# Graph network in four layers: the leaky step of the attention scores on ScalarE, products of high parts first on TensorE, and GpSimd's bias additions held until the aj columns

## The chip, the cores and the metric

The kernel runs on one core of a Trainium2 chip. The metric is the device time of one execution in microseconds (us), as the median of several runs. Engines are named as in the profile: PE (TensorE, matmul), PEld (its weight loads), DVE (VectorE), ACT (ScalarE), POOL (GpSimd), SP (SyncE, which issues the DMAs here).

## The reference

16 graphs of 1024 nodes with 256 features, a dense float32 matrix `adj` of 1024 x 1024 for each, and four layers, each followed by a layer norm of x plus its result:

```python
# layer 0 touches the first 25 nodes of each graph (five small groups), before the loop
# layer 1: attention; z = x @ W.T + bW
ai = z @ wai.T + bai; aj = z @ waj.T + baj          # one number per node each
e = ai + aj.T                                       # 1024 x 1024
e = where(e >= 0, e, 0.2 * e)                       # the leaky step
att = where(adj > 0, e, -9e15)
att = softmax(concat([att, -1e9]), -1)[:, :n]       # a sink column beside the row
x = layernorm(x + att @ z)
# layer 2: x = layernorm(x + relu(((1 + eps) * x + adj @ x) @ W1 + b1) @ W2 + b2)      hidden 512
# layer 3: x = layernorm(x + silu(rmsnorm((eps * x + adj @ x) @ W1 + b1)) @ W2 + b2)   hidden 1024
```

## The kernel before, in words

Each engine has its own program, written out by hand in `layers`, and they meet through semaphores. Every engine runs its instructions in order, so an instruction that waits holds all that stand behind it. Graphs are done one after another in `graph(b, ...)`; the attention scores of graph b + 1 are computed while PE works on layers 2 and 3 of graph b.

Nodes are tiled in 8 tiles of 128 (`NT`), features in 2 (`DT`), and the 1024 nodes of an output in two halves of 512 (`h`). For nearly float32 results most operands are split into a high part (rounded to `F32R`, taken by ACT, or by POOL for some tiles) and a low part (the rest, subtracted by DVE or POOL), and a product is three matmuls: high x high, high x low, low x high. `agg_step` (L755 to L757) adds tile k of `adj @ x` to two banks, `hidden_tile` (L795) makes one 128-wide tile of a hidden layer, `second_step2` (L806) and `second_step3` (L820) multiply the hidden tiles by W2 of layers 2 and 3. A half goes through agg (bank), `agg_hi` on ACT (`a_hi`), `agg_lo` on DVE (`a_lo`, L1276), hidden tiles, then in layer 2 `relu` on ACT (L1006), the second step, then `residual`, `statistics`, `normalize` on DVE with `rstd_of` on POOL, then `x_high` on ACT (L990) and `x_low` on POOL (L1141), which the next layer's aggregation waits for. Two banks hold hidden tiles, so tile m waits for the relu (layer 2) or the squares (layer 3) of tile m - 2.

The scores of graph b + 1 start with `attention_sums` on DVE (L1327, two sums per tile, the last four tiles right after the normalization of the second half) and `attention_columns`, which gives the columns aj (L1333) and ai. PE's `aj_rows` (L733) turns aj into rows in two banks, `aj_copy` (L1269, L1270) copies them and 0.2 times them to SBUF. For each of 8 row tiles `score_mask` (L1343) makes the mask of the adj tile into `neg_mask`, which is the memory of `scratch`; one instruction (L1355) makes the leaky step, max(0.2 aj + shift, aj), with ai taken out of the row; L1360 adds the mask and takes the row maximum; `negated_top` (L1367) negates it with the floor; ACT's `exp` (L994) follows, and PE's `turn_att` (L706) transposes the result. The order on DVE around it is: aj_copy, three rows of scores, `agg_lo` of layer 2's second half, and the other rows between the residuals, statistics and normalizations of layer 2.

On POOL, `add_bias` (L1147) adds layer 2's bias to x, in the order: x_low of tiles 4 to 7, add_bias of tiles 0 to 3, `diag_gap` (L1173, the diagonal for layer 3), add_bias of 4 to 7, `diag_lo` (L1177) twice. ACT's `diag_hi` (L986) stands between; relu of the second half waits for diag_lo, whose source has the same memory.

Of the kernel before, what the change touches and what calls it, by code (L numbers as in the profile page):

```python
# [11 lines left out]
P = 128  # L12
# [438 lines left out]
def layers(nc, sb, sem, banks, ident, ones, WT_hi, WT_lo, W12_hi, W12_lo, W13_hi, W13_lo,  # L451
# [26 lines left out]
    neg_mask = scratch  # L478
# [6 lines left out]
    aj_row, aj_row2 = sb("aj_row", [P, NODES]), sb("aj_row2", [P, NODES])  # L485
# [6 lines left out]
    shift, floor = sb("shift", [P, NT]), sb("floor", [P, NT])  # L492
# [35 lines left out]
    s_sums, s_ai, s_aj, s_shift = sem("attention_sums"), sem("ai_columns"), sem("aj_columns"), sem("shift_and_floor")  # L528
# [85 lines left out]
    with nc.Block() as block:  # L614
# [81 lines left out]
        def _(pe):  # L696
# [44 lines left out]
            def x_ready(b, layer, k):  # L741
                pe.wait_ge(s_x_lo, x_count(b, layer - 1, k))

            def agg_step(b, layer, k, h, second_bank=None, ds=range(DT)):
# [3 lines left out]
                for d in ds:  # L748
# [7 lines left out]
                    nc.tensor.matmul(dst[:], hi, mt_lo[:, k, cols], start=False, stop=False)  # L756
                    mm = nc.tensor.matmul(dst[:], lo, mt_hi[:, k, cols], start=False, stop=done)  # L757
# [5 lines left out]
            def a_ready(b, layer, h):  # L763
                pe.wait_ge(s_a_lo, DT * agg_count(b, layer, h))

# [18 lines left out]
            def hidden_tile(b, layer, h, m):  # L784
# [7 lines left out]
                cols = slice(m * P, (m + 1) * P)  # L792
                for d in range(DT):
                    for n, (l, r) in enumerate(((w_hi, a_hi), (w_hi, a_lo), (w_lo, a_hi))):
                        mm = nc.tensor.matmul(hid_bank[i % 2][:], l[:, d, cols], r[:, d, :], start=(d == 0 and n == 0),  # L795
                                              stop=(d == DT - 1 and n == 2))
# [14 lines left out]
            def second_step3(b, h, m):  # L811
# [3 lines left out]
                pe.wait_ge(s_hid_lo[h], b * HT3 + m + 1)  # L815
                hi, lo = hid_hi[:, m % 4, :], hid_lo[:, m, :]
                for t in HALF_TILES:
                    cols = slice(t * P, (t + 1) * P)
                    for n, (l, r) in enumerate(((hi, W23_hi), (hi, W23_lo), (lo, W23_hi))):
                        mm = nc.tensor.matmul(out_bank[t // 2][:, t % 2 * D:(t % 2 + 1) * D], l[:, cols], r[:, m, :],  # L820
                                              start=(m == 0 and t % 2 == 0 and n == 0),
                                              stop=(m == HT3 - 1 and t % 2 == 1 and n == 2))
                    if m == HT3 - 1 and t % 2 == 1:
                        mm.then_inc(s_out, 1)
# [26 lines left out]
            def graph(b, first, last):  # L851
# [46 lines left out]
                for h in range(2):  # L898
                    a_ready(b, 2, h)
# [13 lines left out]
                a_ready(b, 3, 0)  # L913
# [14 lines left out]
                a_ready(b, 3, 1)  # L928
# [19 lines left out]
        def _(act):  # L948
# [88 lines left out]
            def graph(b, buf, first, last):  # L1037
# [32 lines left out]
                for m in range(HT2):  # L1070
                    relu(b, 0, m)
                    if m == 0:
                        diag_hi(b, 1)
                agg_hi(b, 2, 1)
                if not last:
                    for t in range(2):
                        exp(b + 1, t)
                for m in range(HT2):
                    relu(b, 1, m)
                    if m == 0 and not last:  # L1080
                        exp(b + 1, 2)
                for t in tiles(0):
                    x_high(b, 2, t, buf)
                if not last:
                    exp(b + 1, 3)
                    exp(b + 1, 4)
                for t in tiles(1):
                    x_high(b, 2, t, buf)
                if not last:
                    exp(b + 1, 5)  # L1090
# [27 lines left out]

            for t in range(NT):
                exp(0, t)  # L1120
# [11 lines left out]
        def _(pool):  # L1132
# [51 lines left out]
            def graph(b, buf, first, last):  # L1184
# [28 lines left out]
                for t in tiles(1):  # L1213
                    x_low(b, 1, t, buf)
                for t in range(NT):
# [35 lines left out]
        def _(dve):  # L1251
# [13 lines left out]
            def aj_copy(b):  # L1265
                for i in range(2):
                    dve.wait_ge(s_turned[i], turn_aj_use(b) + 1)
                    cols = slice(i * HALF, (i + 1) * HALF)
                    nc.vector.tensor_copy(aj_row[:, cols], turn_bank[i][:])  # L1269
                    nc.vector.tensor_scalar(aj_row2[:, cols], turn_bank[i][:], SLOPE, None, ALU.mult)\  # L1270
                      .then_inc(s_turn_free[i], 1)
# [60 lines left out]
            def attention_columns(b):  # L1332
                nc.vector.tensor_scalar(aj[:], qj[:], c_cols[:, 1:2], None, ALU.add).then_inc(s_aj, 1)  # L1333
                nc.vector.tensor_scalar(ai[:], qi[:], c_cols[:, 0:1], None, ALU.add).then_inc(s_ai, 1)
                dve.wait_ge(s_ai, b + 1)
                nc.vector.tensor_scalar(shift[:], ai[:], SLOPE - 1.0, None, ALU.mult)
                nc.vector.tensor_scalar(floor[:], ai[:], -1.0, SINK, ALU.mult, ALU.add).then_inc(s_shift, 1)

            def score_mask(b, t):
                dve.wait_ge(s_att_in[t], (b + 1) * 16)  # L1340
                if t > 0:
                    dve.wait_ge(s_masked, b * NT + t)
                nc.vector.tensor_scalar(neg_mask[:], att[:, t, :], 0.0, MASKED, ALU.is_le, ALU.mult).then_inc(s_mask, 1)  # L1343

            def scores(b, t, masked=False):

                if not masked:
                    score_mask(b, t)
                own = att[:, t, :]
                if t == 0:  # L1350
                    dve.wait_ge(s_shift, b + 1)
                    for i in range(2):
                        dve.wait_ge(s_turn_free[i], turn_aj_use(b) + 1)
                dve.wait_ge(s_mask, b * NT + t + 1)
                nc.vector.scalar_tensor_tensor(out=own, in0=aj_row2[:], scalar=shift[:, t:t + 1],  # L1355
# [213 lines left out]
```

## Time and profile before

| | |
|---|---|
| median of 3 runs | 2935.29 us (2935.02 to 2937.99) |
| the profiled execution | 2933.81 us, span 2932.0 us |
| PE busy | 2720.4 us, 93% |
| DVE busy | 2271.9 us, 77% |
| ACT busy | 1433.9 us, 49% |
| POOL busy | 1316.1 us, 45% |
| mean granted clock of PE | 0.973 |

The span is from the first to the last instruction. A busy share is that of the span in which the engine executes. The waits of PE for other engines show what lies beside its work.

### The profile page before, as it was taken

The numbers are of one execution on the slowest core, as the hardware profiler recorded it, in microseconds if no ns is written. First come the engines' busy times: TensorE is split into PE (matmuls) and PEld (weight loads), VectorE is DVE, ScalarE is ACT, GpSimd is POOL, SyncE is SP. The second block draws the span as 40 slices with busy tenths as digits, with TensorE's granted clock in tenths as the row PEclk, the third lists the DMA queues.
The fourth block names the chain that finished last, engine by engine and source line by source line (L and its number), as shares of the span: only waits on it lengthen the run. The fifth ranks groups of instructions, "written<-read, shape, count | busy, mean of one in ns | idle before, by whom it ended". The sixth has DMA issues, their size and how long they took to land.

```text
span 2932.0 us, 41513 instructions
## 1 busy us (share of the span) xinstructions
PE 2720.4 (93%) x14794; PEld 2292.7 (78%) x14794; DVE 2271.9 (77%) x4709; ACT 1433.9 (49%) x2772; POOL 1316.1 (45%) x1392
## 2 busy tenths in 40 slices
PE   3819999999999999999999999999999999999997
PEld 3707787888878787887878788887878788787886
DVE  3265889797878879787887979788887979788734
ACT  0223463746455473646456374645547364544624
POOL 1103455444535544454545544463554435454442
PEclk8958999999999999999999999999999999999999
DMA  4024031120404022030403112040402203040200
GB/s 139 1 78 129 1 110 35 57 88 1 144 1 144 1 80 65 21 124 1 144 1 105 41 52 93 1 144 1 144 1 79 66 19 126 1 144 1 65 9 15
DMA packets 205502, 181.06 MB, mean 62 GB/s; under 512 B 17617, under 2 KB 186993, under 8 KB 205297
## 3 DMA queue, kind: packets, MB, share of 16 engines
q1 hardware_dynamic: 197728, 177.06, 18.8%
q10 hardware_dynamic: 7568, 1.34, 0.3%
q8 instruction: 119, 1.95, 0.3%
q14 instruction: 87, 0.70, 0.1%
HBM read 161.17 MB, written 17.19 MB: 61 GB/s over the span
## 4 chain that ended last, share of the span: by engine, by line
PE 41%; DVE 38%; ACT 6%; issue 6%; POOL 2%; DMA 1%; SPq 0%; DVEq 0%; POOLq 0%; ACTq 0%
PE bank L795 12%; PE bank L820 8%; DVE stat L1304 5%; PE bank L755 5%; PE bank L757 4%; PE bank L756 4%; DVE att L1355 4%; DVE att L1360 4%; PE bank L706 3%; DVE sq_sum L1327 3%; DVE x_even L1319 3%; DVE x_odd L1319 3%; DVE mt_lo L1262 2%; DVE scratch L1343 2%; POOL rstd L1136 2%
## 5 line engine op out<-in xcount | busy, mean ns | idle before, releaser
L755 PE MATMUL bank<-mt_hi,x_hi 128*128 128x512 f32 x1536 | 639.7, 416 | 1.8
L757 PE MATMUL bank<-mt_hi,x_lo 128*128 128x512 f32 x1536 | 606.5, 395 | 0.0
L756 PE MATMUL bank<-mt_lo,x_hi 128*128 128x512 f32 x1536 | 604.6, 394 | 0.0
L1136 POOL TENSOR_TENSOR rstd<-ve,neg_half 128x4 f32<-128x4 f32 x128 | 147.6, 1153 | 499.3 <-DVE ve L1312 499.3
L755 PEld LDWEIGHTS bank<-mt_hi,x_hi 128*128 128x128 f32 x1536 | 291.9, 190 | 77.9 <-POOL x_lo L1141 20.9
L757 PEld LDWEIGHTS bank<-mt_hi,x_lo 128*128 128x128 f32 x1536 | 291.0, 189 | 65.4
L1388 DVE TENSOR_TENSOR sq_sum<-sq_sum,scratch 128x512 f32<-128x512 f32 x224 | 154.7, 691 | 232.1 <-ACT scratch L1025 232.1
L756 PEld LDWEIGHTS bank<-mt_lo,x_hi 128*128 128x128 f32 x1536 | 292.7, 191 | 49.5
L795 PE MATMUL bank<-a_hi,W_hi 128*128 128x512 f32 x768 | 319.5, 416 | 11.9 <-DVE a_lo L1276 11.4
L820 PE MATMUL bank<-W_hi,hid_hi 128*128 128x256 f32 x1024 | 294.7, 288 | 24.8 <-DVE hid_lo L1392 19.1
L795 PE MATMUL bank<-a_hi,W_lo 128*128 128x512 f32 x768 | 304.4, 396 | 0.0
L994 ACT ACTIVATE att<-att,neg_top 128x1024 f32<-128x1024 f32 x128 | 147.2, 1150 | 320.9 <-DVE neg_top L1367 319.9
L795 PE MATMUL bank<-a_lo,W_hi 128*128 128x512 f32 x768 | 304.1, 396 | 0.0
L820 PE MATMUL bank<-W_hi,hid_lo 128*128 128x256 f32 x1024 | 286.7, 280 | 0.0
L820 PE MATMUL bank<-W_lo,hid_hi 128*128 128x256 f32 x1024 | 286.4, 280 | 0.0
L1141 POOL TENSOR_TENSOR x_lo<-x_even,x_hi 128x256 fp32r<-128x256 f32 x192 | 181.3, 959 | 209.1 <-ACT x_hi L990 209.1
L963 ACT ACTIVATE mt_hi<-bank 128x512 fp32r<-128x512 f32 x256 | 153.4, 599 | 245.3 <-PE bank L720 245.2
L1141 POOL TENSOR_TENSOR x_lo<-x_odd,x_hi 128x256 fp32r<-128x256 f32 x192 | 178.1, 942 | 166.0 <-ACT x_hi L990 165.9
L1016 ACT ACTIVATE hid<-bank,b 128x512 f32<-128x512 f32 x256 | 176.4, 689 | 149.0 <-PE bank L820 103.6
L1262 DVE TENSOR_TENSOR mt_lo<-bank,mt_hi 128x512 fp32r<-128x512 f32 x256 | 173.0, 684 | 72.9 <-ACT mt_hi L963 72.8
L1030 ACT ACTIVATE hid<-hid 128x512 f32<-128x512 f32 x256 | 161.2, 630 | 137.2 <-DVE hid L1404 135.5
L806 PE MATMUL bank<-W,hid 128*128 128x256 f32 x1024 | 226.2, 379 | 0.0
(150 smaller groups left out, 6253.4 us busy)
## 6 DMA issues: line engine op xcount, KB each, us to landing
att<-in_adj SPq DMA_DIRECT2D x128, 512.0 KB, 7.8
adj_col<-in_adj SPq DMA_DIRECT2D x256, 256.0 KB, 3.0
out<-x_even SPq DMA_DIRECT2D x64, 128.0 KB, 2.9
out<-x_odd SPq DMA_DIRECT2D x64, 128.0 KB, 2.8
x_even<-in_x SPq DMA_DIRECT2D x56, 128.0 KB, 4.7
x_odd<-in_x SPq DMA_DIRECT2D x56, 128.0 KB, 3.7
G<-in_L_gnn_W SPq DMA_DIRECT2D x2, 2560.0 KB, 14.2
W_f<-in_L_gnn_W SPq DMA_DIRECT2D x1, 1024.0 KB, 8.6
```

What stands on the lines that cost most here:

```text
L755: nc.tensor.matmul(dst[:], hi, mt_hi[:, k, cols], start=k == 0, stop=False)
L756: nc.tensor.matmul(dst[:], hi, mt_lo[:, k, cols], start=False, stop=False)
L757: mm = nc.tensor.matmul(dst[:], lo, mt_hi[:, k, cols], start=False, stop=done)
L795: mm = nc.tensor.matmul(hid_bank[i % 2][:], l[:, d, cols], r[:, d, :], start=(d == 0 and n == 0), stop=(d == DT - 1 and n == 2))
L806: mm = nc.tensor.matmul(out_bank[t // 2][:, t % 2 * D:(t % 2 + 1) * D], src[:, t * P:(t + 1) * P], W22[:, m, :], start=(m == 0 and t % 2 = ...
L820: mm = nc.tensor.matmul(out_bank[t // 2][:, t % 2 * D:(t % 2 + 1) * D], l[:, cols], r[:, m, :], start=(m == 0 and t % 2 == 0 and n == 0), ...
L1016: nc.scalar.activation(hid[:, m, :], src, ACT.Identity, bias=b13[:, m:m + 1])
L1030: nc.scalar.activation(h_m, h_m, ACT.Silu).then_inc(s_silu, 1)
L1136: nc.gpsimd.tensor_tensor(rstd[:, norm, own], ve[:, norm, own], neg_half[:, 0:4], ALU.pow)\
L1141: nc.gpsimd.tensor_tensor(x_lo[:, t, :], x_bufs[buf][:, t, :], x_hi[:, t, :].bitcast(F32), ALU.subtract).then_inc(s_x_lo, 1)
L1262: nc.vector.tensor_tensor(mt_lo[:, k, cols], turn_bank[i][:], mt_hi[:, k, cols].bitcast(F32), ALU.subtract).then_inc(s_turn_free[i], 1)
L1319: nc.vector.tensor_scalar(own, own, mv[:, t, 0:1], rstd[:, layer, t:t + 1], ALU.subtract, ALU.mult).then_inc(s_y[layer], 1)
```

## The change

The leaky step leaves DVE: ACT computes it with Prelu from the aj row and the ai column, after DVE has made the mask, and writes it over the adj tile. The 0.2-times copy of the aj row goes, and its memory becomes a second mask buffer, so masks run two rows ahead. ai stays in the row, so `shift` and `floor` go. The orders of DVE and ACT are written anew around it. On PE, the wait for `x_lo` moves to the first product that reads it, hidden tiles do the products of `a_hi` first (w_lo, w_hi, for both feature tiles) and those of `a_lo` last, and layer 3's second step does the products of `hid_hi` for all four node tiles, and then those of `hid_lo`. On POOL, the additions of layer 2's bias wait for the aj columns of the next graph, and the diagonal steps move between them.

```diff
-    neg_mask = scratch
-    aj_row, aj_row2 = sb("aj_row", [P, NODES]), sb("aj_row2", [P, NODES])
+    aj_row, scratch2 = sb("aj_row", [P, NODES]), sb("scratch2", [P, NODES])
+    masks = [scratch, scratch2]
-    shift, floor = sb("shift", [P, NT]), sb("floor", [P, NT])
...
             def x_ready(b, layer, k):
-                pe.wait_ge(s_x_lo, x_count(b, layer - 1, k))
+                pe.wait_ge(s_x_hi, x_count(b, layer - 1, k))
             def agg_step(...):
                     nc.tensor.matmul(dst[:], hi, mt_lo[:, k, cols], start=False, stop=False)
+                    if d == ds[0]:
+                        pe.wait_ge(s_x_lo, x_count(b, layer - 1, k))
                     mm = nc.tensor.matmul(dst[:], lo, mt_hi[:, k, cols], start=False, stop=done)
+            def a_high(b, layer, h, d):
+                pe.wait_ge(s_a_hi, DT * agg_count(b, layer, h) - 1 + d)
             def hidden_tile(b, layer, h, m):
+                if m == 0 and h == 0:
+                    pe.wait_ge(s_a_lo, DT * agg_count(b, layer, h) - 1)
                 for d in range(DT):
-                    for n, (l, r) in enumerate(((w_hi, a_hi), (w_hi, a_lo), (w_lo, a_hi))):
-                        mm = nc.tensor.matmul(...)
+                    if m == 0:
+                        a_high(b, layer, h, d)
+                    nc.tensor.matmul(dst, w_lo[:, d, cols], a_hi[:, d, :], start=d == 0, stop=False)
+                    nc.tensor.matmul(dst, w_hi[:, d, cols], a_hi[:, d, :], start=False, stop=False)
+                if m == 0:
+                    a_ready(b, layer, h)
+                for d in range(DT):
+                    mm = nc.tensor.matmul(dst, w_hi[:, d, cols], a_lo[:, d, :], start=False, stop=d == DT - 1)
             def second_step3(b, h, m):
-                pe.wait_ge(s_hid_lo[h], b * HT3 + m + 1)
+                pe.wait_ge(s_hid_hi[h], b * HT3 + m + 1)
                 for t in HALF_TILES:
-                    for n, (l, r) in enumerate(((hi, W23_hi), (hi, W23_lo), (lo, W23_hi))):
+                    for n, r in enumerate((W23_hi, W23_lo)):
+                        nc.tensor.matmul(... hi[:, t * P:(t + 1) * P], r[:, m, :], ...)
+                pe.wait_ge(s_hid_lo[h], b * HT3 + m + 1)
+                for t in HALF_TILES:
+                    mm = nc.tensor.matmul(... lo[:, t * P:(t + 1) * P], W23_hi[:, m, :], ...)
...
+            def leaky(b, t):
+                act.wait_ge(s_mask, b * NT + t + 1)
+                if t == 0:
+                    act.wait_ge(s_ai, b + 1)
+                    for i in range(2):
+                        act.wait_ge(s_turn_free[i], turn_aj_use(b) + 1)
+                nc.scalar.activation(att[:, t, :], aj_row[:], ACT.Prelu, bias=ai[:, t:t + 1], alpha=SLOPE)\
+                  .then_inc(s_leaky, 1)
 # ACT, graph(): after agg_hi(b, 2, 0), diag_hi(b, 0); in the last graph without leaky and exp
-                relu 0, diag_hi(b, 1), relu 1, relu 2, relu 3, agg_hi(b, 2, 1), exp 0, exp 1
-                relu 0, exp 2, relu 1, relu 2, relu 3, x_high 0 to 3, exp 3, exp 4
-                x_high 4 to 7, exp 5, exp 6, agg_hi(b, 3, 0), exp 7
+                relu 0, diag_hi(b, 1), leaky 0, relu 1, leaky 1, relu 2, leaky 2, relu 3, exp 0
+                agg_hi(b, 2, 1), leaky 3, exp 1, leaky 4
+                relu 0, relu 1, exp 2, relu 2, leaky 5, relu 3, exp 3, x_high 0 to 3
+                exp 4, leaky 6, exp 5, leaky 7, x_high 4 to 7, exp 6, agg_hi(b, 3, 0), exp 7
 # ACT, before the loop
+            leaky(0, 0)
             for t in range(NT):
+                if t + 1 < NT:
+                    leaky(0, t + 1)
                 exp(0, t)
 # POOL, graph()
+                if not last:
+                    pool.wait_ge(s_aj, b + 2)
                 for t in range(NT):
                     add_bias(b, 1, t, buf)
+                    if t == 0:
+                        diag_gap(b, 1)
+                        diag_lo(b, 0)
                     if t == 3:
-                        diag_gap(b, 1)
-                for h in range(2):
-                    diag_lo(b, h)
+                        diag_lo(b, 1)
 # DVE
             def aj_copy(b):
-                    nc.vector.tensor_copy(aj_row[:, cols], turn_bank[i][:])
-                    nc.vector.tensor_scalar(aj_row2[:, cols], turn_bank[i][:], SLOPE, None, ALU.mult)...
+                    nc.vector.tensor_copy(aj_row[:, cols], turn_bank[i][:]).then_inc(s_turn_free[i], 1)
             def attention_columns(b):
-                nc.vector.tensor_scalar(shift[:], ai[:], SLOPE - 1.0, None, ALU.mult)
-                nc.vector.tensor_scalar(floor[:], ai[:], -1.0, SINK, ALU.mult, ALU.add).then_inc(s_shift, 1)
             def score_mask(b, t):
-                if t > 0:
-                    dve.wait_ge(s_masked, b * NT + t)
-                nc.vector.tensor_scalar(neg_mask[:], ...)
+                if t >= 2:
+                    dve.wait_ge(s_masked, b * NT + t - 1)
+                nc.vector.tensor_scalar(masks[t % 2][:], att[:, t, :], 0.0, MASKED, ALU.is_le, ALU.mult)...
             def scores(b, t):
-                nc.vector.scalar_tensor_tensor(out=own, in0=aj_row2[:], scalar=shift[:, t:t + 1],
-                                               in1=aj_row[:], op0=ALU.add, op1=ALU.max).then_inc(s_leaky, 1)
+                dve.wait_ge(s_mask, b * NT + t + 1)
                 dve.wait_ge(s_leaky, b * NT + t + 1)
                 nc.vector.tensor_tensor_reduce(out=own, in0=own, in1=masks[t % 2][:], ..., op1=ALU.max, ...)
 # DVE, graph(); T is negated_top, M score_mask, S scores
-                aj_copy, M0 S0, M1 S1 (T0), M2 S2 (T1), agg_lo(b, 2, 1), T2, residual and statistics 0
-                M3, normalize 0, S3, M4 S4 (T3), residual and statistics 1
-                M5, normalize 1, S5 (T4), M6 S6 (T5), M7 S7 (T6), T7
+                aj_copy, M0, M1, S0, M2, T0, S1, M3, T1, S2, M4, T2, agg_lo(b, 2, 1), S3, M5, T3
+                residual and statistics 0, S4, normalize 0, T4, M6, S5, M7, T5
+                residual and statistics 1, S6, normalize 1, T6, S7, T7
```

## Rows read from the trace of the kernel before

**Rows 1.** The page: busy time and share of the span, by engine.
```profile
PE 2720.4 (93%) x14794; PEld 2292.7 (78%) x14794; DVE 2271.9 (77%) x4709; ACT 1433.9 (49%) x2772; POOL 1316.1 (45%) x1392
```
**Rows 2.** Waits, whole span: us in total, times, longest us.
```profile
PE bank L733 <- DVE aj L1333: 63.4, 16, 32.5
...
PE bank L706 <- ACT att L994: 31.1, 1, 31.1
...
PEld bank L755 <- POOL x_lo L1141: 20.9, 45, 0.5
...
PE bank L820 <- DVE hid_lo L1392: 19.1, 16, 1.2
...
PE bank L795 <- DVE a_lo L1276: 11.4, 8, 1.5
```
**Rows 3.** Timeline of PE: start us, us, instruction, [idle before <-releaser].
```profile
1304.91 1.09 PE L733 MATMUL bank<-ident,aj 128*128 128x128 f32 x8 [2.05 <-DVE aj L1333]
...
1307.23 0.39 PE L795 MATMUL bank<-a_hi,W_hi 128*128 128x512 f32 x1
...
1312.83 0.38 PE L806 MATMUL bank<-W,hid 128*128 128x256 f32 x1
...
1321.38 0.50 PE L795 MATMUL bank<-a_hi,W_hi 128*128 128x512 f32 x1 [1.48 <-DVE a_lo L1276]
...
1333.79 0.58 PE L755 MATMUL bank<-mt_hi,x_hi 128*128 128x512 f32 x1
```
**Rows 4.** Timeline of DVE: sums of the first graph, of a later one.
```profile
170.05 0.42 DVE L1327 SCALAR_TENSOR_TENSOR sq_sum<-x_even,v_rows 128x256 f32<-128x256 f32 x1
...
1297.04 0.83 DVE L1327 SCALAR_TENSOR_TENSOR sq_sum<-x_odd,v_rows 128x256 f32<-128x256 f32 x1
...
1303.75 1.10 DVE L1333 TENSOR_SCALAR aj<-qj,c_cols 128x8 f32<-128x8 f32 x1
```
**Rows 5.** Timeline of POOL: four bias additions in one row.
```profile
1299.87 3.55 POOL L1147 TENSOR_TENSOR x_even<-x_even,b_row 128x256 f32<-128x256 f32 x4
```
**Rows 6.** Windows: busy us of each engine, granted clock of PE, DMA.
```profile
1474.00:1477.00 3.00, 3.00 (x9) 2.35 (x8) 3.00 (x6) 0.00 (x0) 0.00 (x0) 0.51 0.00 0
```
**Rows 7.** Timeline of DVE: score rows in the first graph and a later one.
```profile
184.38 0.69 DVE L1343 TENSOR_SCALAR scratch<-att 128x1024 f32<-128x1024 f32 x1
...
187.89 0.69 DVE L1343 TENSOR_SCALAR scratch<-att 128x1024 f32<-128x1024 f32 x1
...
1309.59 1.28 DVE L1355 SCALAR_TENSOR_TENSOR att<-aj_row,shift 128x1024 f32<-128x1024 f32 x1
1310.91 2.20 DVE L1360 CUSTOM_DVE_ANT_0 att<-att,scratch 128x1024 f32<-128x1024 f32 x1
...
1315.40 1.21 DVE L1360 CUSTOM_DVE_ANT_0 att<-att,scratch 128x1024 f32<-128x1024 f32 x1
...
1320.05 1.28 DVE L1276 TENSOR_TENSOR a_lo<-bank,a_hi 128x512 fp32r<-128x512 f32 x2
```
**Rows 8.** Timeline of ACT in the same stretch.
```profile
1308.83 0.69 ACT L1006 ACTIVATE hid<-bank,b 128x512 f32<-128x512 f32 x1 [8.90 <-PE bank L795]
1309.42 0.62 ACT L986 ACTIVATE mt_hi<-hid 128x512 fp32r<-128x512 f32 x1
...
1313.62 1.08 ACT L980 ACTIVATE a_hi<-bank 128x512 fp32r<-128x512 f32 x2
1314.71 1.28 ACT L994 ACT_TABLE_LOAD   x1
1316.01 1.15 ACT L994 ACTIVATE att<-att,neg_top 128x1024 f32<-128x1024 f32 x1
```
**Rows 9.** Timeline of DVE: the first low part of layer 3's hidden tiles.
```profile
1375.91 0.69 DVE L1392 TENSOR_TENSOR hid_lo<-hid,hid_hi 128x512 fp32r<-128x512 f32 x1 [0.76 <-ACT hid_hi L1035]
```
**Rows 10.** Timeline of PE: the last product of a hidden tile and the next tile's first.
```profile
1360.78 0.40 PE L795 MATMUL bank<-a_hi,W_lo 128*128 128x512 f32 x1
1361.01 0.40 PE L795 MATMUL bank<-a_hi,W_hi 128*128 128x512 f32 x1
```

More of the change, by code:

```diff
@@ L1069, in graph @@
                 diag_hi(b, 0)
[L1070 to L1073, printed above, removed]
+                relu(b, 0, 0)
+                diag_hi(b, 1)
+                if not last:
+                    leaky(b + 1, 0)
+                relu(b, 0, 1)
+                if not last:
+                    leaky(b + 1, 1)
+                relu(b, 0, 2)
+                if not last:
+                    leaky(b + 1, 2)
+                relu(b, 0, 3)
+                if not last:
+                    exp(b + 1, 0)
                 agg_hi(b, 2, 1)
                 if not last:
-                    for t in range(2):
-                        exp(b + 1, t)
+                    leaky(b + 1, 3)
+                    exp(b + 1, 1)
+                    leaky(b + 1, 4)
                 for m in range(HT2):
                     relu(b, 1, m)
-                    if m == 0 and not last:
+                    if m == 1 and not last:
                         exp(b + 1, 2)
+                    if m == 2 and not last:
+                        leaky(b + 1, 5)
+                if not last:
+                    exp(b + 1, 3)
                 for t in tiles(0):
@@ L1084, in graph @@
                 if not last:
-                    exp(b + 1, 3)
                     exp(b + 1, 4)
+                    leaky(b + 1, 6)
+                    exp(b + 1, 5)
+                    leaky(b + 1, 7)
                 for t in tiles(1):
@@ L1089, in graph @@
                 if not last:
-                    exp(b + 1, 5)
                     exp(b + 1, 6)
@@ L1343, in score_mask @@
[L1343 to L1348, printed above, removed]
-                own = att[:, t, :]
[L1350 to L1354, printed above, removed]
-                nc.vector.scalar_tensor_tensor(out=own, in0=aj_row2[:], scalar=shift[:, t:t + 1],
-                                               in1=aj_row[:], op0=ALU.add, op1=ALU.max).then_inc(s_leaky, 1)
-                dve.wait_ge(s_leaky, b * NT + t + 1)
-                if t > 0 and t != 3:
-                    negated_top(b, t - 1)
-                nc.vector.tensor_tensor_reduce(out=own, in0=own, in1=neg_mask[:], scale=1.0, scalar=-3.0e38,
+                if t >= 2:
+                    dve.wait_ge(s_masked, b * NT + t - 1)
@@ L1361, in scores @@
+                nc.vector.tensor_scalar(masks[t % 2][:], att[:, t, :], 0.0, MASKED, ALU.is_le, ALU.mult).then_inc(s_mask, 1)
+            def scores(b, t):
+                dve.wait_ge(s_mask, b * NT + t + 1)
+                dve.wait_ge(s_leaky, b * NT + t + 1)
+                own = att[:, t, :]
+                nc.vector.tensor_tensor_reduce(out=own, in0=own, in1=masks[t % 2][:], scale=1.0, scalar=-3.0e38,
                                                op0=ALU.add, op1=ALU.max, accum_out=top[:, t:t + 1]).then_inc(s_masked, 1)
-                if t == NT - 1:
-                    negated_top(b, t)
@@ L1462, in graph @@
                 if not last:
+                    score_mask(b + 1, 0)
+                    score_mask(b + 1, 1)
                     for t in range(3):
                         scores(b + 1, t)
+                        score_mask(b + 1, t + 2)
+                        negated_top(b + 1, t)
                 agg_lo(b, 2, 1)
                 if not last:
-                    negated_top(b + 1, 2)
+                    scores(b + 1, 3)
+                    score_mask(b + 1, 5)
+                    negated_top(b + 1, 3)
                 residual(b, 2, 0, buf)
@@ L1470, in graph @@
                 if not last:
-                    score_mask(b + 1, 3)
+                    scores(b + 1, 4)
                 normalize(b, 2, 0, buf)
                 if not last:
-                    scores(b + 1, 3, True)
-                    scores(b + 1, 4)
+                    negated_top(b + 1, 4)
+                    score_mask(b + 1, 6)
+                    scores(b + 1, 5)
+                    score_mask(b + 1, 7)
+                    negated_top(b + 1, 5)
                 residual(b, 2, 1, buf)
```

36 lines of the change are left out of this document (16 added, 20 removed).

## Prediction, made before the change was run

> **What bounds the kernel now.** I read the page's busy shares first: PE (TensorE) is busy 93% of the span, DVE (VectorE) 77%, ACT (ScalarE) 49%, POOL (GpSimd) 45% [rows 1]. So the time is PE's work plus PE's waits, and only what shortens a wait of PE counts. The table of waits says which these are [rows 2]. Three of its rows lie in the body and repeat per graph: the aj columns, 63.4 us in 16 times, of which 32.5 is the start (so about 2.05 in each of 15 graphs); hid_lo, 19.1 us in 16 times; a_lo in 8 graphs, 11.4 us. One lies in the start: 31.1 us for the first graph's exponentials. The reader is to see that all four hang on DVE's and ACT's queues around the attention scores.
>
> One graph then, in the timeline of PE [rows 3]: after a 2.05 us wait the aj transposes start at 1304.91, layer 2's hidden tiles at 1307.23, its second step at 1312.83, the other half's hidden tiles at 1321.38 after another 1.48 us, and layer 3's aggregation at 1333.79. I take this graph as the pattern and move its events.
>
> **aj wait (POOL holds).** The eight sums of tiles 4 to 7 run while POOL adds biases. Alone such a sum took 0.42 us, with POOL at work 0.83 and more, and the aj step itself 1.10 [rows 4]; POOL's last four additions cover 1299.87 to 1303.4 [rows 5], where those of the other four tiles and the low parts of x lie ahead. Held until aj is there, they leave DVE free: with its accumulator read and issue a sum is about 0.47, eight are 3.7 from 1296.1 (the normalization ahead of them is also freed), so aj stands at about 1300.1. PE gets there at 1304.91 - 2.05 = 1302.86, so it is 2.7 us early and the wait goes: -2.05. What is late next on POOL: the additions start 5 us later, diag_gap and diag_lo are now put between them (done about 1309.5, where ACT wants them at 1321), and the second half's residual wants the last addition, at about 1313, only when the second step ends, past 1331. POOL has nothing else queued in between; its hold is hidden.
>
> **The clock.** In 8 of the 16 graphs the granted clock falls to about half (0.51 [rows 6]) for 3.4 us right behind the aj wait, that is from 2.4 to 1.2 GHz; a loss of some 1.7. Those are the graphs in which the a_lo wait doesn't show, since PE arrives later. So each graph pays about 1.5 once, as clock or as a_lo wait.
>
> **a_lo wait of the second half.** In the old order DVE runs three masks, three leaky steps and three masked maxima (0.68, 1.28 and 1.21 to 2.20 each) between aj_copy and agg_lo, which starts at 1320.05 [rows 7]; PE's second step would have ended at 1321.38 - 1.48 = 1319.9. The leaky step leaves DVE, and half of aj_copy. I replay the queues, 2.2 earlier: hidden tiles from 1305.0; relu of tile 0 on ACT 1306.6 to 1307.2, diag_hi to 1307.8 (0.62), leaky 0 to 1308.9, relu 1 to 1309.5, leaky 1 to 1310.6, relu 2 to 1311.1, leaky 2 (its mask waits for maximum 0) 1312.2 to 1313.3, relu 3 to 1314.0, table load to 1315.2, exp 0 to 1316.4, a_hi to 1317.5. Prices: relu 0.69, a_hi 1.08 for two, table load 1.28, exp 1.15 with 0.2 for its accumulator [rows 8]. Prelu is in no row: I take exp's 1.15 (same engine, same 1024 elements, a bias column), 1.38 as the higher near value (two relus), and twice exp, 2.3, as the far one. DVE meanwhile: maxima after leaky 0, 1, 2, five masks, agg_lo from 1317.1 to 1318.5. PE: tile 3 needs relu 1, 0.35 late; second step from 1311.0, done at 1317.9. It begins the second half there, 3.5 before 1321.38, with four products of a_hi (0.93) ahead of its wait for a_lo, so a_lo is wanted at 1318.8: the wait goes. Together with the clock: -1.5.
>
> The Trainium skill (ScalarE: Activation LUTs, What ACT_TABLE_LOAD costs) speaks against this order: it counts about 1.38 us of drain beside the load's 1.28. The row doesn't agree: the load starts at 1314.71, where a_hi ends, and exp 1.30 later [rows 8]. By the row a_hi comes in time; by the page it would be 1.4 later and PE would wait about 0.5 per graph, 8 us less gain.
>
> **What ACT's fuller queue costs.** Beside the 0.35, in the second half leaky 3, exp 1 and leaky 4 stand ahead of relu 0: from 1317.5 they end at 1320.9, relu at 1321.5. PE wants it for tile 2 at 1317.9 + 2.85 = 1320.75: 0.8 late. Its second step then runs from 1324.4 to 1331.2, and layer 3 starts there, not at 1333.79. Sum +1.15 per graph. With Prelu at 1.38 it is +1.85; the lower end is 0, if the first tiles run on as they do now.
>
> **Layer 3's x.** x_high of tiles 4 to 7 now waits behind exp 4. In the new order DVE is about 5 us earlier there and PE no longer waits for x_lo ahead of its first two products. The weight loads waited 20.9 us in 45 times for it [rows 2], 1.3 per graph (three tiles); part of that hides under running products, so I take -0.7 (ends 0 and -1.3).
>
> **hid_lo.** Layer 3's second step waits 19.1 / 16 = 1.19 us for hid_lo [rows 2], of which DVE's subtraction is 0.69 [rows 9]; the chain ahead (a_hi, silu's table load, silu, hid_hi) stays. Now the wait is for hid_hi and eight products (8 x 0.12) hide the subtraction: -0.7.
>
> **Waits at nothing.** Every aggregation step and every second step gets one wait more, some 64 per graph. The pitch over a tile boundary with a wait that is already met is 1361.01 - 1360.78 = 0.23, as inside a tile [rows 10], so I price them at 0.
>
> **The start.** DVE's loop there took 187.89 - 184.38 = 3.5 us a row [rows 7]. The new loop is bound by ACT: leaky and exp, 1.06 + 1.24 = 2.3. Eight rows are 18.4 where they were 28, and aj_copy's two dropped halves are 1.2 more; I take -10 of the 31.1 [rows 2] (ends -5 and -11, since semaphore times may add and the clock there changes).
>
> **Sum.** Per graph -2.05 - 1.5 + 1.15 - 0.7 - 0.7 = -3.8; 15 graphs carry a next graph's scores: -57. The last graph's hid_lo -0.7, the start -10: -67.7. The profiled execution had a span of 2932.0 and a time of 2933.81; the median of the runs, 2935.29, lies 1.5 above. 2932.0 - 67.7 = 2864.3, as a median 2867.
>
> **Rivals.**
> *Slower, by table loads.* If Prelu isn't in the set that holds exp, each change between leaky and exp needs a load of 1.28, some 12 per graph. For it: Prelu is nowhere in the trace. Against: relu, copy and exp follow each other with one load [rows 8]. Place: relu 0 of the second half then comes at about 1325.7, PE waits 3.7 for it, and 1.7 in the first half; layer 3 starts about 1.7 later than now, x_high of its second half just in time. Per graph +1.7 - 0.7 + 0.8 (x_low behind it, paced by POOL) = +1.8, x 15 = 27; the start has two loads per row, 8 x (2.3 + 2.56 - 3.5) = +11: about 2974. It decides as soon as more than some four loads stand ahead of that relu. The Trainium skill (ScalarE: Activation LUTs, Table sets) says that cheap functions such as relu are in every set; it doesn't name Prelu. Chance 0.04.
> *Slower, by the added waits.* If a wait that is met costs half a pitch, 0.12, 64 of them are 7.7 per graph: 16 x 7.7 - 67.7 = +55, 2990; it decides from 67.7 / 16 / 64 = 0.066 us each. The equal pitch of [rows 10] speaks against it. For it: the new waits stand inside a step, between two products into one bank, where the trace has none. Chance 0.03.
> *Nothing gained: Prelu costs twice exp.* Then relu 1 is 1.45 late, relu 0 of the second half 3.5, and a_hi 0.9: layer 3 starts 2.2 later than now, with the two -0.7 it is +0.8 per graph; start 8 x (3.5 - 3.5) = 0: 2935 to 2947. Chance 0.04.
> *Half the gain.* aj comes early, but ACT's relus or a_lo are late by 2 us more than replayed (maxima of 2.20 instead of 1.5 [rows 7], Prelu at 1.4): 2867 + 30 = 2897 and up, to 2925. Chance 0.09.
> *Forecast*, 2847 to 2897: chance 0.80. Its ends: without relu delays and with x_lo at its far end, 2867 - 17 - 9, some of which excludes the other, 2847; with Prelu at 1.38 (+10), the drain (+8), x_lo at nothing (+10), 2895.
>
> A difference under 0.2% (6 us) can't be told from none. Faster: 0.80 + 0.09 + 0.01 of the third; same 0.03; slower 0.07. The range holds the forecast alone and leaves out 2 in 10.
>
> **What would show it.** PE's row "waited for aj" at or near 0 in the body and no half-clock stretch behind it; sums of 0.42 in the second half; the layer 2 wait for a_lo gone from PE's list; new waits of PE for relu, 1.1 per graph in two places; hid_lo's row replaced by one for hid_hi of about 0.5 each; an equal count of table loads; Prelu at 1.15. Wrong it goes if Prelu's rows are longer than 1.5 us, if loads multiply, or if DVE, now waiting for ACT in its order, is late with agg_lo.

## Result, and the profile after

The changed kernel took 2835.85 us (median of 4 runs, 2834.32 to 2838.37), the kernel before 2936.35 on the same chip: a ratio of 0.9658 (0.9642 to 0.9675). That is faster, as forecast, but by 100 us and not by 68, and 11 us below the lower end of the range. The profiled execution (span 2836.6 us, time 2838.37) is the slowest of its four and the one of before lies below its median, so between the two traces the difference is 95.4 us; the bridge is made against that.

The page, busy time by engine (answers to [rows 1]):

```profile
PE 2685.7 (95%) x14794; PEld 2292.9 (81%) x14794; DVE 2027.3 (71%) x4517; ACT 1561.6 (55%) x2900; POOL 1273.3 (45%) x1392
```

DVE lost 245 us and ACT gained 128, somewhat under 128 Prelu of 1.15, since these overlap with their neighbours. The table of PE's waits, whole span (us in total, times, longest; answers to [rows 2]):

```profile
PE bank L732 <- DVE aj L1376: 32.7, 1, 32.7
PE bank L705 <- ACT att L1017: 20.3, 1, 20.3
PE bank L833 <- ACT hid_hi L1058: 17.3, 17, 4.4
```

The aj wait is left once, in the start; a_lo is no longer in the table; hid_lo became hid_hi, 12.9 / 16 = 0.8 us per graph and 4.4 at the end. No wait of PE for a relu is in it, though the prediction had two per graph; one of the two is there all the same, as starts that lie further apart (1266.06 below, right behind relu 1, which ends at 1266.00), with an idle time too short for the table. PE's timeline of one graph, as in [rows 3], with more rows:

```profile
1259.32 1.04 PE L732 MATMUL bank<-ident,aj 128*128 128x128 f32 x8
...
1266.06 0.50 PE L804 MATMUL bank<-a_hi,W_lo 128*128 128x512 f32 x1
...
1267.55 0.81 PE L819 MATMUL bank<-W,hid 128*128 128x256 f32 x3
...
1274.27 0.58 PE L804 MATMUL bank<-a_hi,W_lo 128*128 128x512 f32 x1
...
1286.77 0.58 PE L754 MATMUL bank<-mt_hi,x_hi 128*128 128x512 f32 x1
...
1306.04 0.39 PE L804 MATMUL bank<-a_hi,W_lo 128*128 128x512 f32 x1
...
1327.76 0.36 PE L833 MATMUL bank<-W_hi,hid_hi 128*128 128x256 f32 x1 [0.76 <-ACT hid_hi L1058]
```

PE's work is the same, so the lengths between these marks can be set beside those of before (layer 3's hidden tiles began there at 1354.22, its second step at 1376.75):

| stretch | before | after | difference | predicted |
|---|---|---|---|---|
| wait ahead of the aj transposes | 2.05 | 0 | -2.05 | -2.05 |
| aj transposes to layer 2's second step (relu 1) | 7.92 | 8.23 | +0.31 | +0.35 |
| to the second half's hidden tiles (a_lo) | 8.55 | 6.72 | -1.83 | -1.5 |
| to layer 3's aggregation (relu 0 of the second half) | 12.41 | 12.50 | +0.09 | +0.8 |
| to layer 3's hidden tiles (x) | 20.43 | 19.27 | -1.16 | -0.7 |
| to layer 3's second step (hid_hi) | 22.53 | 21.72 | -0.81 | -0.7 |

The sum is -5.45. From the aj transposes of the second graph to those of the sixteenth, 14 periods, it was 2647.30 - 298.57 and is 2556.6 - 286.6: 167.8 and 162.1 each, -5.6, where the prediction had -3.8. The bridge: the 14 periods 78.7, the start up to the second graph's transposes 12.0, and what is left, the end, 4.7: 95.4. The 12.0 has two parts of opposite sign: in this execution the first aj transposes began 3.1 later than before (180.4 and 177.3), and between them and the second graph's 15.1 were gained, of which 10.8 are the wait for the exponentials (31.1 to 20.3) and 2.05 the aj wait of the second graph.

Why the relu of the second half is in time is seen on ACT, in its timeline (answers to [rows 8]):

```profile
1264.28 1.15 ACT L1012 ACTIVATE att<-aj_row,ai 128x1024 f32<-128x1024 f32 x1
1265.32 0.68 ACT L1029 ACTIVATE hid<-bank,b 128x512 f32<-128x512 f32 x1
...
1268.02 1.15 ACT L1012 ACTIVATE att<-aj_row,ai 128x1024 f32<-128x1024 f32 x1 [0.40 <-DVE scratch L1383]
...
1269.76 1.28 ACT L1017 ACT_TABLE_LOAD   x1
1271.06 1.15 ACT L1017 ACTIVATE att<-att,neg_top 128x1024 f32<-128x1024 f32 x1
1272.12 0.19 ACT L1017 ACTIVATION_READ_ACCUMULATOR att<-att,neg_top 128x1 f32 x1
1272.21 1.07 ACT L993 ACTIVATE a_hi<-bank 128x512 fp32r<-128x512 f32 x2
1273.16 1.14 ACT L1012 ACTIVATE att<-aj_row,ai 128x1024 f32<-128x1024 f32 x1
...
1276.39 0.67 ACT L1029 ACTIVATE hid<-bank,b 128x512 f32<-128x512 f32 x1
```

Prelu takes 1.15, as taken. Each instruction starts some 0.1 ahead of the end of the one before it (relu 1 at 1265.32, where Prelu ends at 1265.43); the replay had that overlap in it already, as it put 1.1 for a Prelu and 0.6 for a relu. The second half's relu 0 starts 2.12 after PE's 1274.27; the replay had 3.0 (1320.9 - 1317.9). Most of the difference arises at leaky 2, which waits for its mask on DVE:

```profile
1265.57 1.27 DVE L1389 CUSTOM_DVE_ANT_0 att<-att,scratch 128x1024 f32<-128x1024 f32 x1 [2.24 <-ACT att L1012]
...
1266.95 1.03 DVE L1383 TENSOR_SCALAR scratch<-att 128x1024 f32<-128x1024 f32 x1
```

From the end of leaky 0 (1265.43) to leaky 2 (1268.02) maximum 0 and mask 2 take 2.59; the replay had 3.3 (1308.9 to 1312.2). DVE's sums and aj (answers to [rows 4]):

```profile
1253.43 0.43 DVE L1370 SCALAR_TENSOR_TENSOR sq_sum<-x_odd,v_rows 128x256 f32<-128x256 f32 x1
...
1256.71 0.23 DVE L1376 TENSOR_SCALAR aj<-qj,c_cols 128x8 f32<-128x8 f32 x1
```

aj is 2.4 us ahead of PE (predicted 2.7), and the granted clock in the three us behind the transposes is 1.00 in the windows read (1259 to 1262, 1421 to 1424, 1583 to 1586).

### The profile page after: what moved, and what is told of

Read it like the earlier page. It is cut to its first block, busy times and chain, and to the rows that moved or that the text cites. A ratio compares the mean times of both kernels' runs of the same rounds, so it can differ in the third digit from the quotient of the medians.

```text
span 2836.6 us, 41497 instructions
## 1 busy us (share of the span) xinstructions
PE 2685.7 (95%) x14794; PEld 2292.9 (81%) x14794; DVE 2027.3 (71%) x4517; ACT 1561.6 (55%) x2900; POOL 1273.3 (45%) x1392
## 4 chain that ended last, share of the span: by engine, by line
PE 67%; DVE 15%; ACT 7%; issue 3%; POOL 1%; DMA 1%; SPq 0%; ACTq 0%; DVEq 0%; POOLq 0%
PE bank L754 9%; PE bank L758 9%; PE bank L755 9%; PE bank L819 8%; PE bank L804 6%; PE bank L809 6%; PE bank L805 6%; PE bank L833 5%; PE bank L705 4%; DVE stat L1347 3%; PE bank L837 3%; DVE x_odd L1362 2%; DVE x_even L1362 2%; DVE hid L1431 2%; PE bank L719 2%
## 5 line engine op out<-in xcount | busy, mean ns | idle before, releaser
L1177 POOL TENSOR_TENSOR rstd<-ve,neg_half 128x4 f32<-128x4 f32 x128 | 164.1, 1282 | 437.0 <-DVE ve L1355 435.4
L804 PE MATMUL bank<-a_hi,W_lo 128*128 128x512 f32 x768 | 319.5, 416 | 1.7
L805 PE MATMUL bank<-a_hi,W_hi 128*128 128x512 f32 x768 | 303.3, 395 | 0.0
L833 PE MATMUL bank<-W_hi,hid_hi 128*128 128x256 f32 x1024 | 260.5, 288 | 17.3 <-ACT hid_hi L1058 17.3
L833 PE MATMUL bank<-W_lo,hid_hi 128*128 128x256 f32 x1024 | 252.4, 280 | 0.0
L1319 DVE TENSOR_TENSOR a_lo<-bank,a_hi 128x512 fp32r<-128x512 f32 x192 | 126.3, 686 | 176.3 <-ACT a_hi L993 176.2
L809 PE MATMUL bank<-a_lo,W_hi 128*128 128x512 f32 x768 | 241.7, 396 | 0.0
L1182 POOL TENSOR_TENSOR x_lo<-x_even,x_hi 128x256 fp32r<-128x256 f32 x192 | 163.3, 866 | 154.1 <-ACT x_hi L1003 154.1
L993 ACT ACTIVATE a_hi<-bank 128x512 fp32r<-128x512 f32 x192 | 109.3, 594 | 217.2 <-PE bank L758 212.5
L1182 POOL TENSOR_TENSOR x_lo<-x_odd,x_hi 128x256 fp32r<-128x256 f32 x192 | 161.9, 858 | 125.0 <-ACT x_hi L1003 125.0
```

Source lines behind the costliest of these rows:

```text
L804: nc.tensor.matmul(dst, w_lo[:, d, cols], a_hi[:, d, :], start=d == 0, stop=False)
L805: nc.tensor.matmul(dst, w_hi[:, d, cols], a_hi[:, d, :], start=False, stop=False)
L809: mm = nc.tensor.matmul(dst, w_hi[:, d, cols], a_lo[:, d, :], start=False, stop=d == DT - 1)
L1177: nc.gpsimd.tensor_tensor(rstd[:, norm, own], ve[:, norm, own], neg_half[:, 0:4], ALU.pow)\
L1182: nc.gpsimd.tensor_tensor(x_lo[:, t, :], x_bufs[buf][:, t, :], x_hi[:, t, :].bitcast(F32), ALU.subtract).then_inc(s_x_lo, 1)
```

## Experiments

Twelve kernels were run, each in 3 rounds with the kernel before on the same chip. Medians in us; the ratio is to the kernel before. That kernel's own median was 2932.7 to 2933.0 in these three sets and 2936.35 beside the changed kernel, so differences from the changed kernel (0.9658) are taken from ratios, times 2935, with the medians' beside them where they differ. Lengths between marks of PE are medians over the 14 periods of a trace.

| run | what | median | ratio (95%) |
|---|---|---|---|
| b_hold | before, POOL's hold and order | 2913.83 | 0.9933 (0.9919 to 0.9948) |
| b_pe | before, PE's changes | 2916.96 | 0.9946 (0.9931 to 0.9960) |
| b_hold_pe | before, both | 2894.08 | 0.9869 (0.9852 to 0.9885) |
| a_leaky | before, leaky step on ACT alone | 2895.34 | 0.9877 (0.9863 to 0.9892) |
| a_nohold | after, without POOL's wait | 2841.16 | 0.9683 (0.9669 to 0.9698) |
| a_oldpool | after, POOL's old order | 2877.50 | 0.9813 (0.9795 to 0.9832) |
| a_xlo | after, PE's old wait for x_lo | 2836.78 | 0.9673 (0.9656 to 0.9689) |
| a_hid | after, old order of products | 2850.46 | 0.9721 (0.9706 to 0.9735) |
| a_longer | after, Prelu longer by some 0.4 | 2861.97 | 0.9760 (0.9745 to 0.9775) |
| a_relu | after, diag_hi behind relu 1 | 2830.38 | 0.9652 (0.9638 to 0.9667) |
| a_silu | after, silu's table load early | 2822.57 | 0.9626 (0.9611 to 0.9640) |
| best | both of these | 2819.54 | 0.9615 (0.9601 to 0.9630) |

**The parts alone.** My theory was a sum of independent parts; the rivals were that a part pays only with another.

b_hold, before with:

```diff
+                if not last:
+                    pool.wait_ge(s_aj, b + 2)
                 for t in range(NT):
                     add_bias(b, 1, t, buf)
+                    if t == 0:
+                        diag_gap(b, 1)
+                        diag_lo(b, 0)
                     if t == 3:
-                        diag_gap(b, 1)
-                for h in range(2):
-                    diag_lo(b, h)
+                        diag_lo(b, 1)
```

> The kernel before with POOL's hold and its new order alone. Theory of parts: aj comes 2.7 us ahead of PE, the aj wait goes (2.2 us per graph with its restart), the clock no longer falls behind it, and a_lo stays late by about 1.5 us, since DVE's leaky steps are still ahead of it and POOL's additions now lie on the score rows: 2936 - 15 x 2.2 = about 2903. Rival, that all gain at aj is lost at a_lo until the leaky step leaves DVE: 2930 to 2936.

It gained 19 us, between the two. The aj wait went, but in the table of PE's waits a_lo grew from 11.4 in 8 to 2.1 each in all 16, where 1.5 each had been expected:

```profile
PE bank L795 <- DVE a_lo L1280: 33.7, 16, 2.2
```

and the clock now falls behind this wait in 8 of the 15 graphs; a window just behind one of them (busy us by engine, then granted clock, DMA share and GB/s):

```profile
1147.00:1149.00 2.00, 2.00 (x6) 1.60 (x5) 1.93 (x9) 0.53 (x1) 0.00 (x0) 0.50 0.00 0
```

b_pe, before with `x_ready` on `s_x_hi` and the new orders in `hidden_tile` and `second_step3`:

> The kernel before with PE's changes alone (x_lo waited for at its first product, products of a_hi and hid_hi first). Theory that these hide low parts: 0.7 us at hid_lo in 16 graphs, 0.9 at a_lo in the graphs that wait there, up to 1 at layer 3's x: 2936 - 30 = about 2906. Rival, that the x gain came from the order of ACT's queue and not from PE's wait: about 2916. If waits that are met cost something, it is slower than 2936.

It gained 16, as the rival said: at layer 3 nothing is won by waiting for x_hi instead of x_lo, because x_hi itself is late there, behind exp 4, which waits for DVE:

```profile
1333.70 1.15 ACT L1008 ACTIVATE att<-att,neg_top 128x1024 f32<-128x1024 f32 x1 [7.80 <-DVE neg_top L1381]
```

The two rows of PE's waits that come of it:

```profile
PE bank L755 <- ACT x_hi L1004: 6.4, 12, 0.6
PE bank L759 <- POOL x_lo L1155: 2.6, 12, 0.2
```

PE's stretches say how much was given back: at the start of layer 3's aggregation this kernel stood 0.91 us ahead of the one before (counted from the aj transposes), at its end 0.12 (the same graph of both traces).

b_hold_pe, both edits:

> The kernel before with POOL's hold and PE's changes, the leaky step still on DVE with one mask buffer. Theory of parts: both add, 2936 - 33 - 30 = about 2870, so that the leaky step's move is worth some 35. Rival, that the leaky step's move is needed for the rest to pay: 2900 or more. Rival, that it is worth nothing: 2836.

39 us, 19 + 16 and a little: the two add, but to 39 and not 63, and the leaky step's move is worth some 60 on top (0.9869 to 0.9658), not the 35 that the theory left for it.

a_leaky, after with PE's and POOL's parts undone:

> The changed kernel with PE's and POOL's parts as before: only the leaky step on ACT, the second mask buffer and the new orders of DVE and ACT. Theory that the move is worth 58 (from 2894 with hold and PE's changes to 2836 with all), since it also frees layer 3's x, to which the other parts lost their gain: 2933 - 58 = about 2875, with the aj wait of 2 us still in every graph. Rival, that it too loses at aj what it gains: 2905 or more.

The rival was nearer: 37. Its table of waits still has the aj wait (62.9 in 16, against 63.4 before) and hid_lo, and a_lo once. The clock falls behind the aj wait in 10 of the 15 later graphs, for instance:

```profile
617.00:619.00 2.00, 2.00 (x6) 1.52 (x6) 2.00 (x4) 0.00 (x0) 0.00 (x0) 0.50 0.00 0
```

Its periods show the price: 164.7 to 165.3 us between aj transposes where the clock holds, 166.3 to 166.9 where it falls, 1.6 more. Before, falls and a_lo waits took each other's place, so all periods were alike (167.3 to 168.0): up to the second half's hidden tiles a graph with a fall took as long as one with the wait (16.4 us from the aj transposes, and 16.5).

So parts of 1.3% and 1.2% make 3.4% together: 38 and 36 us against 100, 26 more than their sum. What each part wins ahead of layer 3, the other's late chain takes back: DVE's rows hold x and a_lo when only aj is early, and the aj wait and its clock stay when only DVE's rows are short. The stretch from layer 3's aggregation to its hidden tiles shows the first: 20.42 before, 21.24 in b_pe, 21.25 in b_hold_pe, where PE comes earlier and x doesn't, and 19.28 in a_leaky and in the changed kernel. (It is 19.28 in b_hold too, but there PE reaches layer 3 2.2 later behind its transposes, for the longer a_lo wait.)

**Which part of POOL's change clears aj.** a_nohold drops the wait alone:

```diff
-                if not last:
-                    pool.wait_ge(s_aj, b + 2)
```

> The changed kernel without POOL's wait for the aj columns, its new order kept. Theory: the sums take 0.83 us and more again, aj is late by about 2 us, 15 x 2.2 = +33, and the clock falls in some graphs (up to +1.7 each): 2869 to 2895. Rival, that aj's slack comes from other parts of the change: 2836.

My theory fell: it cost 7 us (5 by the medians), not 33, and the two ratios' intervals overlap a little. In the trace PE waits for aj again in 10 graphs, at most 0.3 each, and the period is 0.18 longer, some 3 us in all. POOL's timeline shows why so little is lost:

```profile
1250.76 0.79 POOL L1188 TENSOR_TENSOR x_even<-x_even,b_row 128x256 f32<-128x256 f32 x1
1251.50 1.36 POOL L1214 TENSOR_TENSOR hid<-hid,gapI 128x512 f32<-128x512 f32 x1
1255.61 1.49 POOL L1218 TENSOR_TENSOR mt_lo<-hid,mt_hi 128x512 fp32r<-128x512 f32 x1 [2.75 <-ACT mt_hi L999]
```

diag_lo now stands ahead of seven of the eight additions and waits 2.75 us for ACT, so POOL is quiet while DVE sums: the order is itself a hold. The new theory was tried by a_oldpool, which puts POOL's whole part back:

> The changed kernel with POOL's order of before: no wait for aj, diag_gap behind the fourth addition and both diag_lo at the end. Theory from the run without the wait (2841): not the wait but the new order clears the sums, as diag_lo stands ahead of seven additions and waits for ACT; so with the old order the aj wait of 2 us returns, and the clock falls behind it in half of the graphs (1.7 each): 2836 + 31 + 14 = about 2880. Rival, that neither matters any more: 2841.

45 us came back (42 by the medians), as expected, though the clock fell in 5 of 15 graphs and not in half. The waits for aj are 64.9 in 16 again, and DVE's timeline has the long sums:

```profile
1266.84 0.84 DVE L1366 SCALAR_TENSOR_TENSOR sq_sum<-x_odd,v_rows 128x256 f32<-128x256 f32 x1
...
1273.55 1.10 DVE L1372 TENSOR_SCALAR aj<-qj,c_cols 128x8 f32<-128x8 f32 x1
```

**PE's part, in the changed kernel.** a_xlo puts the wait for x_lo back ahead of each step:

```diff
             def x_ready(b, layer, k):
-                pe.wait_ge(s_x_hi, x_count(b, layer - 1, k))
+                pe.wait_ge(s_x_lo, x_count(b, layer - 1, k))
...
-                    if d == ds[0]:
-                        pe.wait_ge(s_x_lo, x_count(b, layer - 1, k))
```

> The changed kernel with PE waiting for x_lo ahead of a whole step again. Theory that x comes in time since ACT's queue has x_high ahead of fewer late exps and DVE is early: no difference, 2834 to 2840. Rival, that PE's later wait made the gain at layer 3's x: 15 x 0.7 = +10, 2846.

No difference that can be told: the medians are 1 us apart, the intervals of the ratios overlap, and PE's mean periods are 162.22 and 162.14. So the 1.16 us at layer 3's x doesn't come from PE's later wait: it came with the leaky step's move and ACT's and DVE's orders, as a_leaky has it whole (19.28). And the 50 waits per graph that this takes away, one for each call of `agg_step`, cost nothing that can be measured. That speaks against the rival of the added waits for this part of them; those of `second_step3` weren't tried alone.

a_hid puts the order of the products back:

> The changed kernel with the products of hidden tiles and of layer 3's second step in their old order, and the waits for a_lo ahead of them. Theory: 0.7 us at hid_lo in 16 graphs and 0.2 to 0.9 at a_lo return: 2836 + 11 + 3 to 14 = 2850 to 2861. Rival, that the slack of the other parts covers it: 2836.

15 us by the medians, 18 by the ratios. PE starts the second half's hidden tiles 0.3 us later, wins some of it back, and loses 0.72 on the way to layer 3's second step, where it stands 0.95 behind in all; hid_lo's wait is back at 19.0 in 16. It lies in the range that was expected, at its lower end.

**ACT's slack.** a_longer:

```diff
...
+                nc.scalar.activation(spare[:], aj_row[:, 0:256], ACT.Prelu, bias=ai[:, t:t + 1], alpha=SLOPE).then_inc(s_spare, 1)
                 nc.scalar.activation(att[:, t, :], aj_row[:], ACT.Prelu, bias=ai[:, t:t + 1], alpha=SLOPE)
```

> The changed kernel with a second Prelu over 256 of the 1024 elements, into a spare buffer, ahead of each leaky step; it adds some 0.4 to ACT's queue each time and changes nothing of the result. Theory that ACT's queue is just in time at relu 1 of the first half and relu 0 of the second: 3 x 0.4 + 2 x 0.4 ahead of the latter, 0.4 ahead of the former, so up to +2 per graph, +5 to +30: 2841 to 2866. Rival, that ACT still has slack: 2836 plus 3 at the start.

26 us (30 by the ratios), and the wait that the prediction had put into the changed kernel appears, in PE's timeline behind relu 1 of the first half and relu 0 of the second:

```profile
1273.85 0.50 PE L805 MATMUL bank<-a_hi,W_lo 128*128 128x512 f32 x1 [0.51 <-ACT hid L1033]
...
1286.39 0.50 PE L805 MATMUL bank<-a_hi,W_lo 128*128 128x512 f32 x1 [1.17 <-ACT hid L1033]
```

So the place of the second wait was right and only the time was off: in the changed kernel that relu ends 2.79 behind the start of the second half's hidden tiles, about when PE wants it (2.85 by the prediction), and with 0.4 us more per leaky step it ends 4.26 behind. Its hidden tiles then take 7.21 us and not 5.78.

**A faster kernel.** a_relu:

```diff
                 relu(b, 0, 0)
-                diag_hi(b, 1)
                 if not last:
                     leaky(b + 1, 0)
                 relu(b, 0, 1)
+                diag_hi(b, 1)
```

> The changed kernel with ACT's diag_hi of the second half moved from ahead of leaky 0 to behind relu 1. Theory that relu 1 is what PE waits 0.35 us for in each graph: 15 x 0.35 = -5, 2831. Rival, that the next relu or a_hi is late by as much: 2836.

a_silu:

```diff
-                agg_hi(b, 3, 1)
+                agg_hi(b, 3, 1, range(1))
+                if b:
+                    act.wait_ge(s_silu, hid3_count(b - 1, 1, HT3 - 1))
+                nc.scalar.activation(spare[:], ones[:], ACT.Silu)
+                agg_hi(b, 3, 1, range(1, 2))
                 silu(b, 0, 0)
 # DVE
-                agg_lo(b, 3, 1)
+                agg_lo(b, 3, 1, range(1))
                 scale_hidden(b, 0, 0)
+                agg_lo(b, 3, 1, range(1, 2))
                 scale_hidden(b, 0, 1)
```

> The changed kernel with a Silu of two columns on ACT between the two a_hi of layer 3's second half, so that the table load lies in ACT's idle time there, and the first scale_hidden ahead of the second a_lo on DVE. Theory that hid_hi is late by this chain: the wait of 12.9 us in 16 graphs goes for the most part, 2836 - 10 = about 2826. Rival, that the row of rms factors is late as well: 2834 or more.

a_relu is 5.5 us faster by the medians but 2 by the ratios, whose intervals overlap. PE's marks show both the theory and its rival: the first half's hidden tiles take 5.60 us as before the change, and not 5.98, so relu 1 did cost PE 0.38; the second half's hidden tiles start 0.38 earlier as well, but take 6.10 and not 5.78, because their relu 0, further down ACT's queue, comes no earlier (it ends 17.72 and 17.74 behind the aj transposes). Only 0.05 is left at their second step. What ACT won ahead of leaky 2 it loses there, waiting for mask 2: POOL's diag_lo, which waits for the moved diag_hi, now runs beside that mask, which takes 1.60 us on DVE, where it took 1.03 in the changed kernel and 0.69 in a_oldpool with POOL idle:

```profile
1260.43 1.60 DVE L1383 TENSOR_SCALAR scratch<-att 128x1024 f32<-128x1024 f32 x1
```

a_silu gained 13 us (9 by the ratios), and PE's marks have it in one place: layer 3's second step starts 0.72 earlier, and 0.9 is won over the period (162.1 to 161.3). The load lies now between the two a_hi, where ACT was idle for 1.67 us in the changed kernel; whether DVE's new order has a share wasn't tried apart:

```profile
1317.59 0.60 ACT L994 ACTIVATE a_hi<-bank 128x512 fp32r<-128x512 f32 x1
1318.20 1.28 ACT L1144 ACT_TABLE_LOAD   x1
1319.50 0.20 ACT L1144 ACTIVATE spare<-ones 128x2 f32<-128x2 f32 x1
1319.83 0.60 ACT L994 ACTIVATE a_hi<-bank 128x512 fp32r<-128x512 f32 x1
```

and of hid_hi's 17 waits only that of the end, 4.4 us, is left.

best, both edits:

> Both of these together, the move of diag_hi and the early table load: 2836 - 5 - 10 = about 2821.

2819.54 us, 3.8% less than the kernel before. It isn't clearly apart from a_silu (periods of 161.2 and 161.3); the two beat the changed kernel by 9 to 16 us.

## Where the prediction was right, and where it failed

- **Direction and places held**: the aj wait, the a_lo wait, x and hid_lo each gained where it was said; no new wait took over. But the gain was 95.4 us between the traces and not 67.7. The rivals with table loads and with a Prelu of 2.3 us are excluded by the trace (14 and 15 loads as before, Prelu 1.15), and a_xlo speaks against the one with costly met waits.
- **The step that failed is "What ACT's fuller queue costs", +1.15 per graph**, the largest error of the sum: some 0.75 x 15 = 11 us. Of its two terms, relu 1's 0.35 was right: the first half's hidden tiles take 5.98 us and not 5.60, and a_relu takes these 0.38 off. The other, relu 0 of the second half at 0.8, was nothing: those hidden tiles take 5.78 and not 5.70, and the same 5.78 in a_oldpool, where that relu ends 0.3 earlier. The replay had the relu end 3.6 behind their start (1317.9 to 1321.5), too late by 0.8; it ended 2.79 behind. The main cause is the step over DVE ahead of leaky 2, maximum 0 and mask 2: 3.3 us from leaky 0's end in the replay and 2.59 in the trace; how the replay came to 3.3 it doesn't say. The rest is 0.2 or less at other rows of the queue, against which PE itself was 0.2 earlier. That the queue is just in time is shown from the other side by a_longer and a_relu, where the relu ends 4.26 and 3.15 behind and PE waits.
- **"Layer 3's x", -0.7, was -1.16**. I took half of the weight loads' 1.3 for hidden. In the trace before, the products' starts lie 0.30 to 0.34 further apart at each of the three tiles, 0.94 in all with the restarts, and 0.1 more ahead of layer 3's hidden tiles. 7 us.
- **"a_lo wait", -1.5, was -1.83**: I booked the idle time of the row, 1.48, but the stretch between the marks was longer by another 0.35, the restart behind it (behind an idle time the first products start further apart). 5 us. The period shows as much as 0.15 that lies in none of the stretches and may be the same at the aj wait, 2 us.
- **"The start", -10**: the exponentials' wait fell by 10.8, which is what the terms of that paragraph add up to (28 - 18.4 + 1.2).
- **"aj wait (POOL holds)"**: the size was right, but the reason was not the wait that I named, so the right size is luck in part. The new order of diag_lo would have done nearly all (a_nohold, a_oldpool).
- **The clock**: that it holds once the wait is gone was right in the traces. That each graph pays "1.5 once, as clock or as a_lo wait" is also what the periods show; I didn't see that it makes the parts worth more together than apart.
- **hid_lo**, -0.7: -0.81, 2 us. The wait for hid_hi is 0.8 each, where 0.5 was expected.
- The drain that the Trainium skill counts beside a table load (ScalarE: Activation LUTs, What ACT_TABLE_LOAD costs) is again not seen: the load starts at 1269.76, where relu 3 ends, and exp 1.30 later.
- **The range.** Its lower end had 17 us for no relu delay and 9 for x at its far end, less something for exclusion. The delays fell short by 11 and x by 7, and these two alone would have stayed inside. The restart behind the a_lo wait, the 2 us of the period, and those of hid_lo were in no bound, and the medians differ by 5 us more than the two traces.

The terms above add up to some 28 us, and 95.4 - 67.7 is 27.7.

What stays open: the 5 us between the medians' difference (100) and the profiled executions' (95) have no row. The start may hold them, as it differs by some 5 us from one execution to another: the first aj transposes lie at 175 to 181 us in these traces, and in that of the changed kernel 3.1 later than before.

## What to carry to other kernels

When you replay queues that wait for each other, write down each term of a wait that crosses from one engine to another (here maximum 0 and mask 2 between two leaky steps); where an engine is just in time, 0.7 us there decides whether a wait exists, and a third engine can lengthen it (mask 2 beside POOL). A wait costs its idle time and the restart behind it, so measure stretches between marks of equal work. When several chains are late near each other, undoing one part at a time tells of their interplay (38 + 36 became 100), and an instruction that waits can hold back what stands behind it, for good as well as for ill.

## What the runs showed of the hardware

- Behind an idle time of PE of 2.04 to 2.23 us in the body the granted clock fell from 2.4 to 1.2 GHz (0.50 in the windows) for 3.4 us in some graphs and not in others: 8 of 15 in the kernel before and in b_hold, 10 in a_leaky, 5 in a_oldpool, 3 in b_pe, at 1.6 us each (a_leaky's periods). The longer idle times didn't bring more falls: those of a_leaky are 2.04 to 2.07, those of b_pe 2.07 to 2.23; what decides between the graphs no run here shows. Behind idle times of 0.8 to 1.5 us no fall was seen in the body of any of these traces.
- A sum on DVE with two SBUF inputs takes 0.43 us alone and 0.84 to 1.39 beside a POOL subtraction or addition (a_oldpool, a_nohold), and even a step of 8 columns goes from 0.23 to 1.10 (changed kernel, a_oldpool). A mask over 1024 elements took 0.69 alone, 1.03 and 1.60 with POOL at work (a_oldpool, changed kernel, a_relu).
- Prelu with a bias column and a slope costs what exp costs, 1.15 us for 1024 elements, and needs no table load of its own beside exp or silu: it runs on both sides of the load at 1269.76, and the counts of loads are unchanged.
